# FFN products over 512 moving columns; edge types by DMA, three buffers of relation rows, later sums, one wait per group of gathers

## The reference, cut to what matters

```python
def _mgcn_conv(x, edge_index, edge_type, rel, W_in, W_out, W_loop, b, n):
    src, dst = (edge_index[0], edge_index[1])
    e = edge_index.shape[1]
    half = e // 2
    m = x[src] * rel[edge_type]
    m = jnp.concatenate([m[:half] @ W_in, m[half:] @ W_out], 0)
    deg = jax.ops.segment_sum(jnp.ones((e,), x.dtype), dst, num_segments=n)
    norm = 1.0 / jnp.maximum(deg, 1.0)
    agg = jax.ops.segment_sum(m * norm[dst][:, None], dst, num_segments=n)
    return jnp.tanh(agg + x @ W_loop + b)
...
h = emb + res * _mgcn_conv(emb, edge_index, edge_type, rel1, W_in1, W_out1, W_loop1, b1, num_nodes)
h = h + res * _mgcn_conv(h, edge_index, edge_type, rel2, W_in2, W_out2, W_loop2, b2, num_nodes)
return h @ mu_w + mu_b
...
# FFN: two experts are chosen for all nodes together, from the mean over the nodes
h = gelu(x @ W1[e] + b1[e]); y = h @ W2[e] + b2[e]     # 256 -> 512 -> 256, for both experts
out = layernorm(w_0 * y_0 + w_1 * y_1 + x)
```

## Time and profile before

| | us |
|---|---|
| median of 3 runs | 2799.32 (2798.51 to 2800.11) |
| the profiled execution | 2798.56 |
| its span, first to last instruction | 2796.8 |

### The profile page before, as it was taken

The page is one execution under the profiler, slowest core; times in us unless marked ns, Lnnn a source line. Parts: engine busy times, 40 slices in busy tenths (PEclk is TensorE's granted clock), DMA queues, the critical chain, the costliest instruction groups (busy, mean ns, idle before and its releaser), DMA issues. The chain is left out here.

```text
span 2796.8 us, 56641 instructions
## 1 busy us (share of the span) xinstructions
PE 2659.6 (95%) x20688; PEld 2513.3 (90%) x20688; DVE 2446.3 (87%) x4506; ACT 1875.4 (67%) x3179; POOL 1928.0 (69%) x2129
## 2 busy tenths in 40 slices
PE   4999999999999998889999999999999988969998
PEld 3999999999999998889999999999999988969998
DVE  6899999999999998978999999999999988975665
ACT  6677766666666665776766666666666656864443
POOL 7777777777777776547777777777777767952222
PEclk9999999999999999999999999999999999989999
DMA  7533333333333333443333333333333334541222
GB/s 240 179 106 106 106 106 106 106 106 106 106 106 106 106 106 102 133 156 105 106 106 106 106 106 106 106 106 106 106 106 106 106 106 134 160 134 57 68 69 68
DMA packets 162469, 312.66 MB, mean 112 GB/s; under 512 B 34061, under 2 KB 95309, under 8 KB 162229
## 3 DMA queue, kind: packets, MB, share of 16 engines
q0 software_dynamic: 79872, 218.21, 26.8%
q1 hardware_dynamic: 81120, 89.89, 9.9%
q10 hardware_dynamic: 1237, 1.41, 0.2%
HBM read 263.90 MB, written 45.48 MB: 111 GB/s over the span
## 5 line engine op out<-in xcount | busy, mean ns | idle before, releaser
L740 PE MATMUL edge_rg<-edge_rel_hi,edge_hot 128*128 128x256 f32 x6656 | 1505.7, 289 | 32.6 <-DVE edge_m_hi L707 12.4
L740 PE MATMUL edge_rg<-edge_rel_lo,edge_hot 128*128 128x256 f32 x4992 | 1271.0, 283 | 0.0
L740 PEld LDWEIGHTS edge_rg<-edge_rel_hi,edge_hot 128*128 128x128 f32 x6656 | 1186.1, 192 | 91.2 <-DVE edge_hot L605 59.4
L740 PEld LDWEIGHTS edge_rg<-edge_rel_lo,edge_hot 128*128 128x128 f32 x4992 | 957.7, 192 | 0.0
L542 ACT CAST edge_m_hi<-edge_rg 128x1024 fp32r<-128x1024 f32 x416 | 422.9, 1016 | 485.2 <-DVE edge_rg L618 485.1
L549 ACT ACTIVATE edge_hot<-edge_typ,minus_type 128x512 fp32r<-128x512 f32 x832 | 527.0, 685 | 168.2 <-PE edge_typ L723 164.7
L605 DVE TENSOR_SCALAR edge_hot<-edge_typ,type_of 128x512 fp32r<-128x512 f32 x832 | 582.8, 743 | 12.5 <-ACT edge_hot L549 8.9
L624 DVE TENSOR_TENSOR edge_m_lo<-edge_rg,edge_m_hi 128x1024 fp32r<-128x1024 f32 x416 | 509.6, 1225 | 87.5 <-ACT edge_m_hi L542 80.8
L531 POOL DMA_INDIRECT work<-h,src x416 | 394.0, 947 | 137.2 <-issue 107.5
L531 POOL DMA_INDIRECT work<-emb,src x416 | 394.5, 948 | 131.2 <-issue 108.1
L531 POOL DMA_INDIRECT edge_xg<-emb,src x416 | 393.5, 946 | 129.7 <-issue 112.7
(11 more groups left out here) (183 smaller groups left out, 3929.0 us busy)
## 6 DMA issues: line engine op xcount, KB each, us to landing
work<-emb,src POOLq DMA_INDIRECT x416, 2.8
edge_xg<-emb,src POOLq DMA_INDIRECT x416
work<-h,src POOLq DMA_INDIRECT x416, 2.8
edge_xg<-h,src POOLq DMA_INDIRECT x416
set_x_rows<-in_x SPq DMA_DIRECT2D x25, 256.0 KB, 3.9
emb<-set_e_rows SPq DMA_DIRECT2D x25, 256.0 KB, 2.9
emb_t<-acc SPq DMA_DIRECT2D x5, 1280.0 KB, 15.7
dense_prev<-emb_t SPq DMA_DIRECT2D x25, 256.0 KB, 2.8
```

Of the source, the lines that this page charges most:

```text
L740: ins = pe.matmul(rg[q % 2][:, t, :], hot[:, q % 2, c, t * P:(t + 1) * P], part[:, c, :], start=(c == 0 and part is rel_hi), stop=(c == FULL))
```

## The change

Edges:

- The setup stores the types as int16 in DRAM (`types`, 104 rows of 1024). PE's spreading matmul is gone; SP loads one row per pair, broadcast over all 128 partitions (256 KB), into one of two SBUF buffers, once the one-hots of two pairs before are made. DVE's and ACT's one-hots read this int16 row in SBUF where they read PSUM.
- `rg` has three PSUM buffers instead of two. DVE's `message` lies 3 turns behind instead of 2, PE's window sums 5 instead of 4, and the transposes and DVE's `add` 6 instead of 4.
- POOL waits once in front of a group, for the message of four groups before, and no longer in front of each gather.

FFN: two chunks are a span of 512 nodes (13 spans, the last with one chunk of 128 columns). `widen` has 512 moving columns. The span is done in four steps of two units; PE's order is narrow of the span before (one step), then widen (one step). The outputs of `narrow` need four PSUM banks. `moments` and `finish` of both chunks of a span come after the whole span's `narrow`.

```diff
+RG_RING = 3
+SUMS_LAG = 5
+TURN_LAG = 6
...
-            act.copy(K["typ"][0:TYPE_ROWS], types_i[0:TYPE_ROWS]).then_inc(tables, 1)
+            act.copy(types_s[0:TYPE_ROWS], types_i[0:TYPE_ROWS]).then_inc(types_short, 1)
+            act.wait_ge(types_short, 1)
+            act.dma_start(types_out, types_s[0:TYPE_ROWS]).then_inc(types_stored, 16)
...
-        pick = s.sb("pick", [P, P], F32R)
+        typ = s.sb("typ", [P, 2, 2 * GROUP * P], I16)
...
-        rg = [s.ps(f"rg{b}", [P, GROUP, DIM]) for b in range(2)]
-        typ = [s.ps(f"typ{b}", [P, GROUP * P]) for b in range(2)]
+        rg = [s.ps(f"rg{b}", [P, GROUP, DIM]) for b in range(RG_RING)]
...
+            def load_types(p):
+
+                wait_past(sp, hot_done, 2 * p - 2)
+                wait_past(sp, distances, HOT_ACT * (2 * p - 2))
+                sp.dma_start(typ[:, p % 2], types[p:p + 1, :].rearrange("o k -> (o k)").partition_broadcast(P))\
+                  .then_inc(typ_in[p % 2], 16)
+
+            load_types(0)
+            load_types(1)
...
+            for p in range(2, PAIRS):
+                load_types(p)
...
+                wait_past(pool, messages, g - GROUPS_IN_RING + 1)
                 for t in range(GROUP):
-
-                    if t < GROUP - 1:
-                        wait_past(pool, rel_tile, (GROUP - 1) * (g - 2) + t + 1)
-                    else:
-                        wait_past(pool, rel_done, g - 1)
                     at = K["src"][:, GROUP * g + t:GROUP * g + t + 1]
...
-                act.wait_ge(typ_done, g + 1)
+                act.wait_ge(typ_in[q // 2], 16 * (i + 1))
+                wait_past(act, rel_done, g - 1)
                 for c in range(HOT_ACT):
-                    act.activation(hot[:, q % 2, c], typ[q % 2][:], ACT.Abs,
+                    act.activation(hot[:, q % 2, c], types_of(q), ACT.Abs,
                                    bias=K["minus_type"][:, c:c + 1]).then_inc(distances, 1)
...
-                over_groups(act, (0, later(distance)), (2, high), (0, later(one_hot)), (3, copy_sums), (0, clear_one))
+                over_groups(act, (SUMS_LAG, copy_sums), (3, high(by_three)), (0, later(distance)), (0, later(one_hot)),
+                            (0, clear_one))
...
-                dve.wait_ge(distances, HOT_ACT * (g + 1))
-
+                dve.wait_ge(typ_in[q // 2], 16 * (i + 1))
+                wait_past(dve, rel_done, g - 1)
                 for c in range(HOT_ACT, RCHUNKS):
-                    ins = dve.tensor_scalar(hot[:, q % 2, c], typ[q % 2][:], K["type_of"][:, c:c + 1], None,
+                    ins = dve.tensor_scalar(hot[:, q % 2, c], types_of(q), K["type_of"][:, c:c + 1], None,
                                             ALU.is_equal)
...
-                over_groups(dve, (2, message), (2, one_window), (4, add_window), (2, low), (0, one_hot_later))
+                over_groups(dve, (3, message(by_three)), (0, one_hot_later), (3, one_window), (TURN_LAG, add_window),
+                            (3, low(by_three)))
...
+                    if q % 2 == 0:
+                        wait_past(pe, added, g // 2 - 1)
...
-                over_groups(pe, (4, one_window), (2, relation_rows), (0, spread_later), (4, turn_over))
+                over_groups(pe, (SUMS_LAG, one_window), (TURN_LAG, turn_over), (2, relation_rows(by_three)))
...
+        STEP = 2
+        STEPS_UP = U // STEP
+        SPAN = 2 * CHUNK
+        SPANS = -(-CHUNKS // 2)
...
-        full = carve(2, U // 2, CHUNK, part=work)
-        hid = [s.sb(f"hid{k}", [P, 2, U, CHUNK], F32R) for k in range(2)]
+        full = work[:, used:used + 2 * STEP * SPAN].rearrange("p (r u n) -> p r u n", r=2, u=STEP)
+        hid = [s.sb(f"hid{k}", [P, U, SPAN], F32R) for k in range(2)]
...
-            over_chunks(dve, (2, moments), (0, low(0)), (2, finish), (0, low(1)), (0, w2_low))
+            for m in range(SPANS + 2):
+                ready = chunks_of(m - 2) if m > 1 else []
+                for q in range(STEPS_UP):
+                    if q < len(ready):
+                        moments(ready[q], ready[q] % 2, ready[q] // 2)
+                    if m < SPANS:
+                        low(m, q)
+                    if 0 <= q - 1 < len(ready):
+                        finish(ready[q - 1], ready[q - 1] % 2, ready[q - 1] // 2)
+                    if m == 0 and q == 1:
+                        dve.wait_ge(w2_split, 1)
+                        dve.tensor_tensor(w2[1], w2_raw, w2[0].bitcast(F32), ALU.subtract).then_inc(w2_split, 1)
...
+            def widen(m, u):
+
+                if m == 0 and u % STEP == 0:
+                    pe.wait_ge(w1_lo, u // STEP + 1)
+                wait_past(pe, gelu_done, U * m + u - 3)
+                out = up[u % 4][:, 0:wide(m)]
+                nodes = slice(2 * m, 2 * m + 2) if len(chunks_of(m)) == 2 else slice(2 * m, 2 * m + 1)
+                each = wide(m) // len(chunks_of(m))
+                out = out.rearrange("p (o n) -> p o n", n=each)
+                for k in range(DC):
+                    ins = product(pe, out, [w[:, u // HC, k, (u % HC) * P:(u % HC + 1) * P] for w in w1],
+                                  [K["ln_parts"][:, part, nodes, k, 0:each] for part in range(2)],
+                                  k == 0, k == DC - 1)
+                ins.then_inc(up_done, 1)
+
...
+            def narrow(m, q):
+
+                pe.wait_ge(hid_lo, STEPS_UP * m + q + 1)
+                if q == 0:
+                    wait_past(pe, y_done, 2 * (m - 1))
+                    if m == 0:
+                        pe.wait_ge(w2_split, 2)
+                for u in units(q):
+                    for h, j in blocks_of(m):
+                        at = slice((2 * h + j) * P, (2 * h + j + 1) * P)
+                        a, b = [v[:, u, at] for v in hid], [w[:, u // HC, u % HC] for w in w2]
+                        out = down[m % 2][h][:, j, :]
+                        for k, (x, z) in enumerate(((1, 0), (0, 1), (0, 0))):
+                            ins = pe.matmul(out, a[x], b[z], start=(u == 0 and j == 0 and k == 0),
+                                            stop=(u == U - 1 and k == 2), skip_group_check=True)
+                if q == STEPS_UP - 1:
+                    ins.then_inc(down_done, 1)
+
+            for m in range(SPANS + 1):
+                for q in range(STEPS_UP):
+                    if m > 0:
+                        narrow(m - 1, q)
+                    if m < SPANS:
+                        for u in units(q):
+                            widen(m, u)
 
         @block.scalar
         def _(act):
...
+            for m in range(SPANS):
+                for q in range(STEPS_UP):
+                    gelu(m, q)
+                    high(m, q)
+                    if m == 0 and q == 1:
+                        act.wait_ge(weighted, 2)
+                        act.copy(w2[0], w2_raw).then_inc(w2_split, 1)
```

217 lines of the change are left out of this document (90 added, 127 removed).

## The result

The changed kernel takes 2818.06 us (median of 4 runs, 2817.05 to 2818.63), the kernel before 2799.72 in the same session (2798.51 to 2801.87): a ratio of 1.0060, 95% interval 1.0048 to 1.0072, 18 us slower. The profiled execution took 2818.38 us, with a span of 2816.3.

The account below looks back on a forecast made before the run. The prediction took POOL's gathers to bound the edges and PE's stream the FFN. Terms 0 + 1 - 1.4 - 5 + 10.4 = +5.0 us gave 2803.6, or 2804 by the median; own range 2796 to 2809, 8 in 10 2793 to 2822.

Parts of the forecast that it names:

- rival A: Edges: the two one-hots shut POOL out and lengthen gathers, 54 to 71 us, 2858 to 2875; 15%, milder forms from 2808.
- the stall: Start of layer 0: POOL's idle time in front of gathers, forecast at 1.8 us in place of 3.2.
- What bounds the kernel: Edges paced by POOL's gathers, 1.25 us start to start; FFN by PE's stream, with a DVE and POOL tail.
- Waits in front of the gathers, 0 in the steady state: Edges: dropping three or four POOL waits a group is worth 0, at most 17 us.
- The one-hots and the port, +1 us: Edges: DVE's new one-hots stretch some gathers in a stage's first 30 groups; +1 us, bounds 0 and 183.
- SP's loads at the start, -1.4 us: Start of layer 0: types of pair 2 land at 89, shortening POOL's idle time; -1.4 us, bounds -3.3 and +5.
- `widen`, -5 us: FFN: one 512-column matmul replaces two of 256, 9 ns saved on each of 528; -5 us, bounds 0 and -13.
- The end, +10.4: FFN's end: a longer chain of `moments`, loads, bias adds and `finish` after the last full span; +10.4 us, bounds +7 and +13.
- D: FFN's end: the end of `narrow` of chunk 23, from which the span was forecast to end 24.0 us later.

Follow-up runs that it names:

- waits_once: The kernel before, with POOL waiting once in front of a group and no longer in front of each gather: 2797.05 us, ratio 0.9988.
- select_first: The changed kernel, with DVE's four selection instructions moved between the message and the two one-hots: 2876.09 us, ratio 1.0274.
- late_stores: The changed kernel, with SP loading the relation matrix first and spreading layer 0's five `emb_t` stores behind the types of pairs 2 to 6: 2812.96 us, ratio 1.0042.
- edges_only: The changed kernel's edges and setup with the FFN of the kernel before: 2809.50 us, ratio 1.0037.

## Why the prediction was right or wrong

The forecast was 2804, with an own range of 2796 to 2809; the run is 2818, 14 us above the forecast and outside that range. It lies in the range of 8 in 10 (2793 to 2822) only because that one left room for milder forms of rival A; no term of the sum gave this time. The sum was +5.0, and the spans differ by 19.5. Of the 14.5 missed the longer gathers are 6.8 (1.7 of it only the median's 1 ns), the stall 5.0 and `widen` 1.3; the rest lies between the stages and in the setup.

- **What bounds the kernel**: right. In all kernels the edges go at POOL's pace, 1.25 us a gather, and dropping PE's and DVE's work paid nothing there.
- **Waits in front of the gathers, 0 in the steady state**: right (waits_once). I missed that the same edit takes the stall of the earlier trace rows away by itself.
- **The one-hots and the port, +1 us**: the step that failed; it cost 6.1. The port is the way to SBUF that the prediction takes DVE and POOL to share. "I take it that it is held up too" was true for the second one-hots that start from 0.48 on (0.60 to 0.72 us in place of 0.48), and not for those before it; and one-hots that run when a gather starts were not thought of at all. A row showed that case: the subtraction that ran at 65.85 ended 0.57 into the gather, which took 1.39; I used it as a bound alone. The gathers over 0.96 cost that much more than before (7.9 less 1.8). The mechanism of rival A was right for a part, and so was its point, "under some 0.5" (measured: 0.48). Of the 7.9 us, 2.8 lie in gathers with a one-hot running at 0.49, which is rival A; 3.4 in gathers that started while a one-hot ran, which no rival had; 1.0 before 110 us. The second one-hot sat at 0.52 to 0.54 in the forecast and at 0.55 in the trace, under 0.1 from the edge, and a quarter of the messages came 35 ns or more ahead of the median. I priced rival A with all groups in it (54 to 71 us), named milder forms without a price, and took the forecast as none; it is a share of the groups. select_first, with most groups in it, cost 58.
- **SP's loads at the start, -1.4 us**: wrong sign, measured +3.6 (POOL's idle time over the usual, 6.7 against 3.2). I asked when the types of pair 2 land (said 89, came at 94.3), and that is the small stall of 0.96. The large one is the message of group 0: behind three one-hot pairs in place of two, behind a matrix split 3.0 us later against the first gather, and behind what I take for a fetch of DVE's code, which the page does not name. late_stores takes it away.
- **`widen`, -5 us**: PE's stream from the first start of widen to the last start of narrow went from 286.3 to 282.6 us, -3.7. The mechanism was right and the merge itself worth what was forecast: matmuls of 512 columns are 230 ns apart in the mean (2532 to 2765 us), two of 256 took 240 before, and 528 x 9.5 ns are 5.0 us. What was left out: the matmuls of `narrow` between them came 120.2 ns apart in the mean where they came 118.6 apart before (some 1.7 us, cause open), and each change from narrow to widen took 125 ns. Up to the first narrow the stream gained 0.6 us, where 0 was forecast.
- **The end, +10.4**: right. From the last narrow's end to the end of the span it is 10.4 us longer (19.75 against 9.3); 24.1 us measured from D, 24.0 forecast, and by the chain of steps forecast: chunk 22's bias adds done at D + 3.9 (3.5), `moments` of 23 at D + 9.5 (8.9), POOL's adds for 24 done at D + 17.8 (17.7).
- From the last gather to the FFN and between the layers, forecast 0: +0.3 and +0.2. Start to first gather, +0.8: edges_only and select_first, with the same setup, start their first gather at 60.42 and 60.35, so this belongs to the execution.

Sum: gathers +7.8 (of it 1.7 the median's 1 ns), stall +3.6, setup +0.8, between the stages +0.5, FFN +6.8: 19.5.

## What to carry to other kernels

Work taken off engines that do not set the pace is free to take, and free to hurt: what counts is where the instructions that are left now fall in the cycle of the engine that does set it. When a forecast rests on a place in a cycle, compare the margin (here under 0.1 us) with the spread of that place, and price the share of cycles that fall outside. A buffer set free helps only if the instruction that fills it is not queued behind another that waits; and of a wait whose named releaser was done long ago, ask what else the engine needs, its code included.

## What the runs showed of the hardware

**Two moments of a gather.** The Trainium skill (SBUF — State Buffer, "Who interferes with whom") has POOL and such DVE instructions exclude each other for the whole instruction, the first one winning. The traces agree that there is an exclusion, but not for the whole instruction: first one-hots that start 0.10 to 0.35 into a gather run beside it and leave it at its 0.946. They show two moments. A gather of 128 rows (0.946 us) is stretched in two ways. If a 512-column int16 one-hot (or the f32 subtraction of the earlier trace rows) runs when the gather starts, the gather ends 0.82 us behind it: one-hot ends at 0.33, gather 1.15; 0.42 and 1.23; the subtraction 0.57 and 1.39. If one runs at 0.49 into it, having started before, the gather ends 0.12 behind it where that is later than 0.946: 0.95 and 1.07; the cast 1.00 and 1.12. One that starts from 0.48 on is held up itself: the second one-hots that started at 0.50 to 0.55 took 669 ns in the mean in place of 481. That POOL writes something at these two moments is my reading; no run shows what.

**It hangs on the operand.** From SBUF as int16, the one-hot takes 483 ns in the median, against 743 in the mean from PSUM as f32, and only the first kind stretches gathers. In the kernel before, the pair of the earlier trace rows at 509.82 runs through both moments of this gather:

```profile
509.87 0.95 POOL L531 DMA_INDIRECT work<-emb,src  x1 [0.30 <-issue]
```

From the 26th group of each layer on, 420 gathers of that trace started with such a one-hot still to run for over 0.13 us (0.946 less 0.82), and none took over 951 ns. Place and type of the operand changed together and were not tried apart; the cast and the subtraction of the earlier trace rows, which stretched gathers too, read f32 from SBUF.

**Code seems to come by DMA, and to queue.** With the DMA engines at 370 to 410 GB/s DVE waited 8.38 us after its branch and 5.38 us at the next piece; with the stores spread it waited 3.75 after the branch, and the next wait (1.90) was one for relation rows. That both waits of the changed kernel are code is inferred: three times DVE went on 1.87 us after an 8 KB packet of an instruction queue had started (77.50, 83.76, and 69.87 in late_stores). The stores and the order of the loads were moved together, and were not tried apart.
